# Third attention layer: raw keys loaded in a head's second step; score operands and value tables of later heads issued by GpSimd

## The chip, the cores and the metric

One core of one Trainium2 chip runs the whole program. The metric is the device time of one execution in microseconds (us). Durations in the traces are in us unless they are marked ns.

## The reference, cut to what is touched

The program is a chain of four attention layers and four feed-forward layers on `x` of shape (4, 512, 128). The change lies in the third attention layer alone, which has 16 heads of 8 channels over 4 batches of 512 tokens, and a bias and a value term that depend on the clipped distance between query and key:

```python
qkv = (x @ w_qkv.T).reshape(B, N, 3, H, hd).transpose(2, 0, 3, 1, 4)
q, k, v = (qkv[0] * scale, qkv[1], qkv[2])
attn = jnp.einsum('bhid,bhjd->bhij', q, k)
idx = rp[None, None]                       # clip(j - i, -31, 31) + 31
qL = jnp.einsum('bhid,hdm->bhim', q, rpe_k_table)
attn = attn + jnp.take_along_axis(qL, idx, axis=-1)
kL = jnp.einsum('bhjd,hdm->bhjm', k * scale, rpe_q_table)
attn = attn + jnp.swapaxes(jnp.take_along_axis(kL, idx, axis=-1), 2, 3)
attn = jax.nn.softmax(attn, axis=-1)
out = jnp.einsum('bhij,bhjd->bhid', attn, v)
S = segment_sum of attn over rp            # 63 sums for each query
out = out + jnp.einsum('inbh,hnd->bhid', S, rpe_v_table)
return x_out @ w_proj.T + b_proj
```

## The kernel before

The layer (`l2_attn`, L2053) has a preparation and then a loop over 16 heads. A head has 8 steps; a step is one pair of blocks of 32 queries, for all 4 batches at once, on 128 partitions. Each engine runs its own program in order, written out by the Python loop over `t` = 8h + i, where h is the head and i the step (0 to 7). The engines are held together by semaphores alone. What each engine does, by step:

- TensorE: `scores(t)` (bf16 parts of queries and keys, 51 rows, at the start of each step), then `key_bands(h + 1, i - 1)` in steps 1 to 3 (the key bias of the next head, from `xk` and `kshift`), `query_bands(h + 3, i - 4)` in steps 4 to 7, the value matmuls of the half head before in three parts, and `relative(n)` (L2708) four steps later.
- VectorE: `maximum(t)` (adds the bias of `qb`, takes the row maximum), `turn` (transposes probabilities), in steps 3 and 7 `turn_band` (L2534, transposes the band `sb` of the half head that ended four steps before step 4 or 0) and `normalize`.
- ScalarE: evacuation of the key and query bands, `exp(t)`, `outputs`.
- GpSimd: `sums` and `cut` (L2474, masks `sb`) every fourth step, `combine(h + 1)` in step 4 (4.7 us of work on `qb`: the DMA-loaded query bias and the key bias `kb` of the next head), `values(h + 1)` in step 5 (the value operand `vd`; waits for the value matmuls of the half head before, whose last part is in TensorE's step 4), `expand(h + 2)` in step 7 (L2457, spreads the raw keys `rawk` into `xk`).
- SyncE issues every DMA of the loop. In its order of a head: `q_load(h + 1)` (skewed read of the query band from HBM into `qb`, 768 KB) and `q_store(h + 2)` (768 KB to HBM) in step 0; `p_store` in steps 0, 2, 4 and 6 (probability bands of two steps to HBM, 736 KB a head, in rows of 384 bytes or less); `s_load` in steps 3 and 7 (L2399, the stored band read back skewed into `sb`, 384 KB each), which first waits until the two stores that it reads have landed; `head_scores(h + 1)` in step 3 (query parts 192 KB, key parts 384 KB, bias rows 24 KB); `keys(h + 2)` in step 4 (raw keys, 8 rows of 8 KB each read 16 times, 1024 KB, and `kshift`, 56 KB); `head_values(h)` in step 5 (48 KB).

The skewed reads have this access pattern, whose outermost dimension is the 4 batches:

```python
def skewed(band, offset, step, width):
    pitch = width + GRP
    return bass.AP(band.tensor, band.offset + offset, [[GRP * pitch, B], [pitch + step, GRP], [1, width]])
```

`keys(h)` waits for `xk_ready` >= h, that is, until `expand(h - 1)` has read the one `rawk` tile. `expand(h)` needs the load and the last key round of head h - 1 (step 3). The first key round of head h + 1, in TensorE's step 1, waits for `expand(h + 1)`. `combine(h + 1)` has to be done when VectorE starts head h + 1.

Of the kernel before, what the change touches and what calls it, by code (L numbers as in the profile page):

```python
# [12 lines left out]
P = 128  # L13
# [4 lines left out]
T = B * NT  # L18
# [4 lines left out]
HEADS, HD = 16, 8  # L23
# [2029 lines left out]
def l2_attn(nc, xs, c, w, scratch):  # L2053
# [4 lines left out]
    with ExitStack() as ctx:  # L2058
# [15 lines left out]
        ps_l = s.ps("ps_l", [P, N])  # L2074
        names = ("w_loaded t_loaded m_loaded rv_loaded zero_ready zeroed wt_ready wT_ready zb_ready t_ready zT_ready qk_ps base_ready hi_ready res_ready "
                 "mid_ready lo_ready q_lo gam_ps gam_ready g_lo g_stored v_ps va_ready tab_ready tab_stored rvd_ready rvd_stored st0 st1 "
                 "ones_ready once_ready hl0 hl1 kl kt0 kt1 rl0 rl1 l_ps l_ready qw0 qw1 qw2 qr0 qr1 pw0 pw1 pw2 sr0 sr1 tabq_ready "
                 "s_ps biased nm_ready p_ready tT xk_ready added comb_ready sm_ready vs_ready masked st_ready vd_ready pv_done o_ps oe_ready u_ps rr_ready o_done "
                 "at_ps aoT_ready y_ps y_ready dve")
        m = {n: s.sem(n) for n in names.split()}  # L2080
        ident = c["ident"]
        head_loaded = [m["hl0"], m["hl1"]]
        shifts_loaded = [m["kt0"], m["kt1"]]
        rv_slot_loaded = [m["rl0"], m["rl1"]]
        qband_read = [m["qr0"], m["qr1"]]
# [242 lines left out]
        with nc.Block() as block:  # L2328
            @block.sync
            def _(sp):  # L2330
# [22 lines left out]
                def head_values(h):  # L2353

                    if h >= 2:
                        sp.wait_ge(m["o_ps"], 2 * h - 2)
                    sp.dma_start(rvt[h % 2][:, :, :].rearrange("p k n -> p (k n)"), rv_d[h]).then_inc(rv_slot_loaded[h % 2], 16)
# [61 lines left out]
                for t in range(L2_STEPS + 4):  # L2419
                    h, i = t // PAIRS, t % PAIRS  # L2420
                    if t % 2 == 0 and 0 <= (t - 2) // 2 < L2_STEPS // 2:
                        p_store((t - 2) // 2)
                    if t % 4 == 3 and 0 <= (t - 7) // 4 < 2 * HEADS:
                        s_load((t - 7) // 4)
                    if i == 0 and h + 1 < HEADS:
                        q_load(h + 1)
                    if i == 0 and 3 <= h + 2 < HEADS:
                        q_store(h + 2)
                    if i == 3 and 2 <= h + 1 < HEADS:
                        head_scores(h + 1)  # L2430
                    if i == 4 and h + 2 < HEADS:
                        keys(h + 2)
                    if i == 5 and 2 <= h < HEADS:
                        head_values(h)

            @block.gpsimd
            def _(g):
                g.memset(ones3[:, :], 1.0).then_inc(m["ones_ready"], 1)
                g.memset(xk[:, 0:GRP], 0.0).then_inc(m["once_ready"], 1)
                g.memset(xk[:, GRP + T * P:], 0.0).then_inc(m["once_ready"], 1)  # L2440
# [52 lines left out]
                for t in range(L2_STEPS + 12):  # L2493
                    h, i = t // PAIRS, t % PAIRS
                    if t % 4 == 1 and 0 <= (t - 5) // 4 < 2 * HEADS:
                        sums((t - 5) // 4)
                    if t % 4 == 2 and 0 <= (t - 10) // 4 < 2 * HEADS:
                        cut((t - 10) // 4)
                    if i == 4 and h + 1 < HEADS:
                        combine(h + 1)  # L2500
                    if i == 5 and 2 <= h + 1 < HEADS:
                        values(h + 1)
                    if i == 7 and h + 2 < HEADS:
                        expand(h + 2)
                ln.powers(g, 2 * B, start=B)

# [123 lines left out]
            def _(pe):  # L2630
# [22 lines left out]
                def scores(g):  # L2653
                    h, slot = g // PAIRS, g % 2
                    if g % PAIRS == 0:
                        pe.wait_ge(head_loaded[h % 2], 16 * (HEAD_LOADS * (h // 2 + 1) + 1))
                    if g >= 2:
                        pe.wait_ge(m["p_ready"], 2 * g - 2)
                    r0 = P // 2 * (h % 2)
                    for u in range(2):  # L2660
                        a = 2 * (g % PAIRS) + u
                        right = GRP * (a - 1) if a else 0
                        for b in range(B):
                            out = ps_s[slot][GRP * b:GRP * (b + 1), u, :]
                            q = qs[r0:r0 + FROWS, b * N + GRP * a:b * N + GRP * (a + 1)]
                            keys = lambda v, lo, hi: ks[r0:r0 + FROWS, v, b * N + lo:b * N + hi]
                            if a == 0:
                                pe.matmul(out[:, 0:GRP], q, keys(0, N - GRP, N), start=True, stop=True)
                                last = pe.matmul(out[:, GRP:N], q, keys(0, 0, N - GRP), start=True, stop=True)
                            else:  # L2670
                                if right:
                                    pe.matmul(out[:, N - right:N], q, keys(1, 0, right), start=True, stop=True)
                                last = pe.matmul(out[:, 0:N - right], q, keys(0, right, N), start=True, stop=True)  # L2673
                    last.then_inc(m["s_ps"], 1)
# [33 lines left out]
                def relative(n):  # L2708
# [1 line left out]
                    h = n // 2  # L2710
                    pe.wait_ge(m["st_ready"], n + 1)
                    if n % 2 == 0:
                        pe.wait_ge(rv_slot_loaded[h % 2], 16 * (h // 2 + 1))
                    for k in range(3):
                        last = pe.matmul(ps_o[n % 2][GRP * k:GRP * (k + 1), :], rvt[h % 2][:, k, :], st[n % 2][:, :, k, :], start=False, stop=True)
                    last.then_inc(m["o_ps"], 1)
# [570 lines left out]
```

## Time and profile before

| | |
|---|---|
| median of 3 runs | 2629.41 us (2624.09 to 2635.16) |
| the profiled execution | 2632.55 us |
| its span, first to last instruction | 2630.6 us |
| mean granted TensorE clock | 0.849 |
| busy in the span: TensorE, VectorE, ScalarE, GpSimd | 1926.2, 1713.3, 1090.8, 847.6 us |
| head loop of this layer | 1610 to 2076 us of the span |

The profiled execution took 1.95 us more than its span. Busy times are shares of the whole program; for a change in one loop the table by stretches of that loop and the waits in it are what to read.

### The profile page before, as it was taken

To read this page: it belongs to the slowest core of one execution; us is meant where nothing else is said; L and a number is where in the kernel's file an instruction comes from. 1 tells how busy PE (TensorE), PEld (TensorE's weight loads), DVE (VectorE), ACT (ScalarE), POOL (GpSimd) and SP (SyncE) were. 2 spreads that over 40 slices of the span, in tenths; PEclk is the share of its full clock that TensorE was granted. 3 is DMA by queue.
4 is the path that set the end of the run, shared out by engine and by line. 5 is a ranking of instruction groups with operands and counts; after the bars stand their busy time and mean duration, and the time that the engine had idled before them with its cause. 6 is when DMAs were issued, how large, how long until landed. Compare 5 with 4: busy or idle time off the path is not lost. (4 is left out here: it accounts for less than half of the span.)

```text
span 2630.6 us, 46533 instructions
## 1 busy us (share of the span) xinstructions
PE 1926.2 (73%) x16472; PEld 1324.4 (50%) x16472; DVE 1713.3 (65%) x4060; ACT 1090.8 (41%) x2021; POOL 847.6 (32%) x627
## 2 busy tenths in 40 slices
PE   4888886387777784559999647787787549995446
PEld 1555554155555553437777524454454338884334
DVE  3777776576555554659999843788888672224564
ACT  1666663254544442204444223555555213331332
POOL 3000000574444421014444334445545169201001
PEclk8999999699999987659999765898988669997667
DMA  3011110210000000010000065566665140000000
GB/s 100 29 38 39 39 39 3 63 27 15 15 15 15 15 15 5 1 21 11 20 20 20 11 192 140 164 177 172 173 173 153 48 175 17 16 0 8 0 1 19
DMA packets 126467, 145.04 MB, mean 55 GB/s; under 512 B 72472, under 2 KB 100171, under 8 KB 123490
## 3 DMA queue, kind: packets, MB, share of 16 engines
q1 hardware_dynamic: 123040, 132.95, 18.1%
q10 hardware_dynamic: 3266, 9.96, 1.0%
q8 instruction: 99, 1.62, 0.3%
q14 instruction: 62, 0.51, 0.1%
HBM read 94.59 MB, written 40.81 MB: 51 GB/s over the span
## 5 line engine op out<-in xcount | busy, mean ns | idle before, releaser
L407 ACT ACTIVATE l0a_pr<-l0a_sm,l0a_nm 128x512 f32<-128x512 f32 x256 | 184.9, 723 | 147.4 <-DVE l0a_nm L324 146.9
L324 DVE CUSTOM_DVE_ANT_0 l0a_sm<-l0a_ps_s,l0a_tb 128x512 f32<-128x512 f32 x256 | 171.0, 685 | 93.9 <-PE l0a_ps_s L473 90.8
L2606 ACT ACTIVATE l2a_pr<-l2a_ps_s,l2a_nm 128x512 f32<-128x512 f32 x256 | 174.1, 687 | 120.8 <-DVE l2a_nm L2525 119.9
L481 PE MATMUL l0a_ps_p<-top_c_ident,l0a_pr 128*128 128x128 f32 x1024 | 170.4, 290 | 54.2 <-ACT l0a_pT L415 54.1
L481 PEld LDWEIGHTS l0a_ps_p<-top_c_ident,l0a_pr 128*128 128x128 f32 x1024 | 110.0, 143 | 117.1 <-ACT l0a_pr L407 64.7
L2525 DVE TENSOR_REDUCE l2a_nm<-l2a_ps_s 128x2 f32<-128x1024 f32 x128 | 156.7, 1224 | 4.4
L2532 DVE STREAM_TRANSPOSE l2a_tt<-l2a_pr 128x1024 f32<-128x1024 f32 x128 | 158.0, 1234 | 0.1
L1508 POOL TENSOR_TENSOR l1f_h<-l1f_lm,l1f_sg 128x512 f32<-128x512 f32 x72 | 92.6, 1286 | 184.0 <-DVE l1f_lm L1577 184.0
L754 POOL TENSOR_TENSOR l0f_ct<-l0f_raw,l0f_cos_scaled 128x1024 f32<-128x1024 f32 x32 | 76.3, 2386 | 184.1 <-issue 94.7
L1880 ACT ACTIVATE l2f_h<-l2f_ps_h 128x512 f32<-128x512 f32 x128 | 76.7, 599 | 134.7 <-PE l2f_ps_h L1425 128.9
L1635 ACT ACTIVATE l1f_csb<-l1f_ps_c,l1f_b3e 128x512 f32<-128x512 f32 x128 | 88.2, 689 | 104.9 <-PE l1f_ps_c L1425 104.6
L1918 PEld LDWEIGHTS l2f_ps_y<-l2f_w2T,l2f_h 128*128 128x128 f32 x1024 | 119.1, 192 | 2.6
L2702 PE MATMUL l2a_ps_o<-l2a_tt,l2a_vd 128*32 128x256 f32 (+7 forms) x1472 | 119.8, 364 | 0.0
L1918 PE MATMUL l2f_ps_y<-l2f_w2T,l2f_h 128*128 128x128 f32 x1024 | 119.3, 275 | 0.0
L1838 DVE SCALAR_TENSOR_TENSOR l2f_acc<-l2f_ps_y,l2f_comb,l2f_acc 128x128 f32<-128x128 f32 x112 | 31.6, 344 | 133.1 <-PE l2f_ps_y L1918 132.9
L990 PE MATMUL l0f_ps_side<-l0f_wqkv,l0f_hT 128*128 128x512 f32 x192 | 109.8, 663 | 11.5 <-ACT l0f_hT L905 10.8
L2523 DVE TENSOR_TENSOR l2a_ps_s<-l2a_ps_s,l2a_qb 128x192 f32<-128x192 f32 (+2 forms) x160 | 45.7, 303 | 106.2 <-PE l2a_ps_s L2673 61.3
L286 POOL COPY l0a_vh<-l0a_va 128x128 f32 x14 | 4.1, 296 | 333.2 <-PE l0a_ps_o L492 333.2
L473 PE MATMUL l0a_ps_s<-l0a_ks,l0a_qs 48*128 48x512 bf16 x256 | 101.7, 398 | 10.1 <-issue 9.5
L2649 PE MATMUL l2a_ps_l<-l2a_xk,l2a_kshift 128*32 128x256 f32 x768 | 71.3, 504 | 48.7 <-POOL l2a_xk L2462 46.2
L770 POOL TENSOR_TENSOR l0f_rn<-l0f_ss,top_c_half 128x16 f32<-128x16 f32 x32 | 95.0, 2968 | 33.1 <-DVE l0f_ss L854 32.1
L2462 POOL TENSOR_TENSOR l2a_xk<-l2a_rawk,l2a_masks 128x2048 f32<-128x2048 f32 x16 | 72.3, 4517 | 66.0 <-DMA l2a_rawk<-l_k 66.0
(501 smaller groups left out, 5220.9 us busy)
## 6 DMA issues: line engine op xcount, KB each, us to landing
l2a_rawk<-l_k SPq DMA_DIRECT2D x16, 1024.0 KB, 13.2
l2a_qb<-l_qband SPq DMA_DIRECT2D x16, 768.0 KB
l2a_sb<-l_pband SPq DMA_DIRECT2D x32, 384.0 KB
l_qband<-l2a_staged SPq DMA_DIRECT2D x14, 768.0 KB, 15.4
l0a_tb<-l_bias SPq DMA_DIRECT2D x16, 448.0 KB
l2a_ks<-l_k SPq DMA_DIRECT2D x16, 384.0 KB
l_pband<-l2a_pr SPq DMA_DIRECT2D x32, 192.0 KB, 9.4
l_pband<-l2a_pr SPq DMA_DIRECT2D x32, 144.0 KB, 2.9
```

What stands on the lines that cost most here:

```text
L324: v.tensor_tensor_reduce(sm[j % 4][:, :], ps_s[j % 2][:, :], tb[slot][:, off:off + N][:, ::-1], -1.0, 3e38, ALU.add, ALU.min, nm[:, j % 4: ...
L407: a.activation(pr[j % 4][:, :], sm[j % 4][:, :], ACT.Exp, bias=nm[:, j % 4:j % 4 + 1], scale=-1.0).then_inc(m["p_ready"], 1)
L473: pe.matmul(ps_s[j % 2][:, :], qs[slot][:, b * N + it * P:b * N + (it + 1) * P], ks[slot][:, b * N:(b + 1) * N], start=True, stop=True).th ...
L481: last = pe.transpose(ps_p[j % 2][:, tile(k)], pr[j % 4][:, tile(k)], ident[:, :])
L770: g.tensor_tensor(rn[:, u, :], ss[:, u, :], c["half"][:, :], ALU.pow).then_inc(m["rn_ready"], 1)
L990: last = pe.matmul(bank[:, :], hT[:, tile(t)], wqkv[:, l, i * F_INNER:(i + 1) * F_INNER], start=True, stop=True)
L1508: g.tensor_tensor(h[b % 2][:, k, :], lm[:, k, :], sg[:, k, :], ALU.mult).then_inc(h_ready, 1)
L1918: last = pe.matmul(ps_y[b % 2][:, t, :], h[b % 2][:, k, t * P:(t + 1) * P], w2T[slot][:, k, :], start=(k == 0), stop=(k == FC - 1))
L2525: v.tensor_reduce(nm[:, g % 2, :], ps_s[g % 2][:, :, :], AX, ALU.max, negate=True).then_inc(m["nm_ready"], 1)
L2532: v.transpose(tt[n % 2][:, u * NB:(u + 2) * NB, :].rearrange("p (u k) i -> p u (k i)", u=2), pr[g // 2 % PR_RING][:, 2 * (g % 2):2 * (g % ...
L2606: a.activation(pr[slot][:, 2 * (g % 2) + u, :], ps_s[g % 2][:, u, :], ACT.Exp, bias=nm[:, g % 2, u:u + 1], accum_out=rs[:, n % 2, 2 * (g % ...
L2702: last = pe.matmul(ps_o[n % 2][GRP * g:GRP * (g + 1), (lo - a0) * GRP:(hi - a0) * GRP], vd[h % 2][:, v, k, :], tt[n % 2][:, block:block + ...
```

## The change

`keys(h + 2)` moves on SyncE from step 4 to step 1. `head_scores` and `head_values` leave SyncE's loop (the calls for heads 0 and 1 ahead of it stay). GpSimd issues the same four transfers for heads 2 to 15: `score_loads(h + 1)` in its step 2 (three DMAs) and `value_load(h)` in its step 4, with semaphores of their own and the same conditions. GpSimd's own work moves too: `values(h + 1)` from step 5 to step 3, `combine(h + 1)` from 4 to 5, `expand(h + 2)` from 7 to 6. TensorE waits for the new semaphores in heads 2 and later.

```diff
@@ -2074,12 +2074,14 @@
         ps_l = s.ps("ps_l", [P, N])
         names = ("w_loaded t_loaded m_loaded rv_loaded zero_ready zeroed wt_ready wT_ready zb_ready t_ready zT_ready qk_ps base_ready hi_ready res_ready "
                  "mid_ready lo_ready q_lo gam_ps gam_ready g_lo g_stored v_ps va_ready tab_ready tab_stored rvd_ready rvd_stored st0 st1 "
-                 "ones_ready once_ready hl0 hl1 kl kt0 kt1 rl0 rl1 l_ps l_ready qw0 qw1 qw2 qr0 qr1 pw0 pw1 pw2 sr0 sr1 tabq_ready "
+                 "ones_ready once_ready hl0 hl1 gh0 gh1 gv0 gv1 kl kt0 kt1 rl0 rl1 l_ps l_ready qw0 qw1 qw2 qr0 qr1 pw0 pw1 pw2 sr0 sr1 tabq_ready "
                  "s_ps biased nm_ready p_ready tT xk_ready added comb_ready sm_ready vs_ready masked st_ready vd_ready pv_done o_ps oe_ready u_ps rr_ready o_done "
                  "at_ps aoT_ready y_ps y_ready dve")
         m = {n: s.sem(n) for n in names.split()}
         ident = c["ident"]
         head_loaded = [m["hl0"], m["hl1"]]
+        later_head_loaded = [m["gh0"], m["gh1"]]
+        later_rv_loaded = [m["gv0"], m["gv1"]]
         shifts_loaded = [m["kt0"], m["kt1"]]
         rv_slot_loaded = [m["rl0"], m["rl1"]]
         qband_read = [m["qr0"], m["qr1"]]
@@ -2426,15 +2428,26 @@
                         q_load(h + 1)
                     if i == 0 and 3 <= h + 2 < HEADS:
                         q_store(h + 2)
-                    if i == 3 and 2 <= h + 1 < HEADS:
-                        head_scores(h + 1)
-                    if i == 4 and h + 2 < HEADS:
+                    if i == 1 and h + 2 < HEADS:
                         keys(h + 2)
-                    if i == 5 and 2 <= h < HEADS:
-                        head_values(h)
 
             @block.gpsimd
             def _(g):
+                def score_loads(h):
+
+                    g.wait_ge(m["s_ps"], PAIRS * (h - 1))
+                    first, sem = P // 2 * (h % 2), later_head_loaded[h % 2]
+                    g.dma_start(qs[first:first + KROWS, :], q3[h * HD:(h + 1) * HD].rearrange("d c t -> (d c) t")).then_inc(sem, 16)
+                    g.dma_start(ks[first:first + KROWS, :, :].rearrange("p v t -> p (v t)"),
+                                k3[h * HD:(h + 1) * HD].rearrange("d c v t -> (d c) (v t)")).then_inc(sem, 16)
+                    src = bass.AP(g3.tensor, g3.offset + h * 3 * T * P, [[T * P, 3], [HEADS * 3 * T * P, 2], [1, T * P]])
+                    g.dma_start(ks[first + KROWS:first + FROWS, :, :], src).then_inc(sem, 16)
+
+                def value_load(h):
+
+                    g.wait_ge(m["o_ps"], 2 * h - 2)
+                    g.dma_start(rvt[h % 2][:, :, :].rearrange("p k n -> p (k n)"), rv_d[h]).then_inc(later_rv_loaded[h % 2], 16)
+
                 g.memset(ones3[:, :], 1.0).then_inc(m["ones_ready"], 1)
                 g.memset(xk[:, 0:GRP], 0.0).then_inc(m["once_ready"], 1)
                 g.memset(xk[:, GRP + T * P:], 0.0).then_inc(m["once_ready"], 1)
@@ -2496,11 +2509,15 @@
                         sums((t - 5) // 4)
                     if t % 4 == 2 and 0 <= (t - 10) // 4 < 2 * HEADS:
                         cut((t - 10) // 4)
-                    if i == 4 and h + 1 < HEADS:
+                    if i == 2 and 2 <= h + 1 < HEADS:
+                        score_loads(h + 1)
+                    if i == 3 and 2 <= h + 1 < HEADS:
+                        values(h + 1)
+                    if i == 4 and 2 <= h < HEADS:
+                        value_load(h)
+                    if i == 5 and h + 1 < HEADS:
                         combine(h + 1)
-                    if i == 5 and 2 <= h + 1 < HEADS:
-                        values(h + 1)
-                    if i == 7 and h + 2 < HEADS:
+                    if i == 6 and h + 2 < HEADS:
                         expand(h + 2)
                 ln.powers(g, 2 * B, start=B)
 
@@ -2653,7 +2670,9 @@
                 def scores(g):
                     h, slot = g // PAIRS, g % 2
                     if g % PAIRS == 0:
-                        pe.wait_ge(head_loaded[h % 2], 16 * (HEAD_LOADS * (h // 2 + 1) + 1))
+                        pe.wait_ge(head_loaded[h % 2], 16 * (HEAD_LOADS + 1))
+                        if h >= 2:
+                            pe.wait_ge(later_head_loaded[h % 2], 16 * HEAD_LOADS * (h // 2))
                     if g >= 2:
                         pe.wait_ge(m["p_ready"], 2 * g - 2)
                     r0 = P // 2 * (h % 2)
@@ -2710,7 +2729,9 @@
                     h = n // 2
                     pe.wait_ge(m["st_ready"], n + 1)
                     if n % 2 == 0:
-                        pe.wait_ge(rv_slot_loaded[h % 2], 16 * (h // 2 + 1))
+                        pe.wait_ge(rv_slot_loaded[h % 2], 16)
+                        if h >= 2:
+                            pe.wait_ge(later_rv_loaded[h % 2], 16 * (h // 2))
                     for k in range(3):
                         last = pe.matmul(ps_o[n % 2][GRP * k:GRP * (k + 1), :], rvt[h % 2][:, k, :], st[n % 2][:, :, k, :], start=False, stop=True)
                     last.then_inc(m["o_ps"], 1)
```

## Rows read from the trace of the kernel before

**Rows 1.** The page's groups of instructions, line engine op, out<-in.

```profile
L2649 PE MATMUL l2a_ps_l<-l2a_xk,l2a_kshift 128*32 128x256 f32 x768 | 71.3, 504 | 48.7 <-POOL l2a_xk L2462 46.2 <-ACT l2a_kb L2592 1.4 <-ACT l2a_pr L2585 0.6
...
L2462 POOL TENSOR_TENSOR l2a_xk<-l2a_rawk,l2a_masks 128x2048 f32<-128x2048 f32 x16 | 72.3, 4517 | 66.0 <-DMA l2a_rawk<-l_k 66.0
```

**Rows 2.** Waits, 1660 to 2060 us: total us, times, longest us.

```profile
PE l2a_ps_s L2668 <- DMA l2a_ks<-l_g: 17.7, 9, 6.7
```

**Rows 3.** Waits of SyncE's queue, 1560 to 2100 us.

```profile
SPq L2403 <- DMA l_pband<-l2a_pr: 65.0, 15, 9.5
```

**Rows 4.** Table by stretches; the last three columns are clock, DMA share, GB/s.

```profile
1669.94:2011.30 341.36, 272.17 (x3952) 159.41 (x3952) 283.02 (x380) 180.12 (x484) 165.75 (x120) 0.87 0.63 173
1678.00:1679.00 1.00, 1.00 (x20) 0.19 (x16) 0.00 (x0) 0.00 (x0) 0.00 (x0) 0.50 0.21 61
1789.00:1790.00 1.00, 0.00 (x0) 0.00 (x0) 1.00 (x2) 0.00 (x0) 1.00 (x1) 0.50 0.98 402
1794.00:1795.00 1.00, 1.00 (x20) 0.36 (x16) 0.37 (x1) 1.00 (x4) 0.00 (x0) 0.50 0.25 104
1832.00:1840.00 8.00, 7.79 (x124) 5.51 (x120) 7.90 (x10) 5.08 (x14) 6.13 (x6) 1.00 0.98 214
```

**Rows 5.** SyncE's timeline over one head: start, duration of the issue.

```profile
1812.99 0.53 SPq L2404 DMA_DIRECT2D l2a_sb<-l_pband  x1
...
1814.68 0.53 SPq L2380 DMA_DIRECT2D l2a_qb<-l_qband  x1
1815.31 1.64 SPq L2373 DMA_DIRECT2D l_qband<-l2a_staged  x1
...
1825.24 0.52 SPq L2404 DMA_DIRECT2D l2a_sb<-l_pband  x1
1825.81 1.43 SPq L2347 DMA_DIRECT2D l2a_qs<-l_q  x1
...
1831.08 0.39 SPq L2397 DMA_DIRECT2D l_pband<-l2a_pr  x1
1831.51 0.57 SPq L2336 DMA_DIRECT2D l2a_rawk<-l_k  x1
...
1837.64 0.37 SPq L2397 DMA_DIRECT2D l_pband<-l2a_pr  x1
1840.97 0.54 SPq L2404 DMA_DIRECT2D l2a_sb<-l_pband  x1
```

**Rows 6.** SyncE's timeline: loads of step 7 of heads 0, 1, 13; a long issue.

```profile
1635.61 0.55 SPq L2404 DMA_DIRECT2D l2a_sb<-l_pband  x1
...
1648.99 7.06 SPq L2347 DMA_DIRECT2D l2a_qs<-l_q  x1
...
1669.94 0.53 SPq L2404 DMA_DIRECT2D l2a_sb<-l_pband  x1
...
2011.30 0.54 SPq L2404 DMA_DIRECT2D l2a_sb<-l_pband  x1
```

**Rows 7.** GpSimd's timeline over the same head as rows 5.

```profile
1829.67 1.28 POOL L2470 TENSOR_TENSOR l2a_qb<-l2a_qb,l2a_masks 128x512 f32<-128x512 f32 x1 [8.63 <-ACT l2a_kb L2592]
1831.03 3.45 POOL L2472 TENSOR_TENSOR l2a_qb<-l2a_qb,l2a_kb 128x1536 f32<-128x1536 f32 x1
...
1834.64 0.72 POOL L2448 TENSOR_TENSOR l2a_vs<-l2a_va,l2a_rvf 128x256 f32<-128x256 f32 x1
1835.44 2.04 POOL L2452 TENSOR_TENSOR l2a_vd<-l2a_vs,l2a_masks 128x512 f32<-128x512 f32 x2
1838.70 0.73 POOL L2477 TENSOR_TENSOR l2a_sb<-l2a_sb,l2a_masks 128x256 f32<-128x256 f32 x1 [1.23 <-DMA l2a_sb<-l_pband]
1843.46 4.52 POOL L2462 TENSOR_TENSOR l2a_xk<-l2a_rawk,l2a_masks 128x2048 f32<-128x2048 f32 x1 [4.02 <-DMA l2a_rawk<-l_k]
```

**Rows 8.** Last head, empty queue: SyncE's issue of a band load.

```profile
2059.19 0.52 SPq L2404 DMA_DIRECT2D l2a_sb<-l_pband  x1
```

**Rows 9.** GpSimd's `cut` that waited for the load of rows 8.

```profile
2066.10 0.73 POOL L2477 TENSOR_TENSOR l2a_sb<-l2a_sb,l2a_masks 128x256 f32<-128x256 f32 x1 [1.72 <-DMA l2a_sb<-l_pband]
```

## The prediction

> **What bounds the kernel now.** I read the groups of instructions first, then the waits of all engines, the waits of SyncE's queue, the table by stretches of 1 us, and last the timelines of SyncE and GpSimd over one head. The groups show what the change seems made for: TensorE stands 46.2 us in front of its key rounds until `expand` is done, and GpSimd stands 66.0 us in front of `expand` until the raw keys have landed [rows 1]. TensorE also waits 17.7 us for the key parts of the scores [rows 2]. SyncE waits 65.0 us in `s_load` for its own stores to land [rows 3]. Three transfers late at once point at the transfers themselves.
>
> The table by stretches gives the reason. A DMA share of 0.25 with 104 GB/s is 4 of the 16 DMA engines at full speed, 26 GB/s each; all sixteen reach 402 GB/s, 25 each [rows 4]. The skewed reads (`q_load`, `s_load`) have 4 as their outermost dimension and show just this share. Over the 390 windows of 1 us from 1645 to 2035 us the share never falls below 0.21; the lowest is shown [rows 4]. So four DMA engines are never idle through heads 1 to 13, while the other twelve often are. Head by head the step-7 `s_load` is issued every (2011.30 - 1669.94) / 12 = 28.45 us [rows 6]. That is the four engines' work of one head. VectorE, the busiest compute engine, has 283.02 / 12 = 23.6 us of work a head in the same stretch [rows 4].
>
> The rule behind the 4 is in the Trainium skill, DMA: Bandwidth & Descriptors, section "Why a DMA increments its semaphore by 16 and not by 1": a transfer is spread over the largest number up to 16 that divides the slowest dimension of both sides. The trace agrees (0.25).
>
> What the four engines move in a head, from the sizes in the text above: a quarter of 768 + 2 x 384 KB = 384 KB, and a sixteenth of 768 + 1024 + 600 + 736 + 56 + 48 = 3232 KB, 202 KB. At 26 GB/s (393 + 207 thousand bytes) this is 15.1 + 8.0 = 23.1 us. The other 28.45 - 23.1 = 5.35 us are lost where all sixteen run at once and well below 402 GB/s: 214 GB/s at a share of 0.98 from 1832 to 1840 us [rows 4], just behind the issue of the raw keys [rows 5].
>
> **The change part by part.** No byte is removed and none is added. The question for each part is thus what it does to four engines that are always busy.
>
> *Raw keys in step 1.* Now they are last in line: issued at 1831.51, 18.5 us into the cycle that begins with the `s_load` at 1812.99, landed at 1843.46, 2.5 us after the next cycle began at 1840.97 [rows 5, 7]. Issued in step 1 they stand right behind `q_store` (1815.31), and land long before GpSimd wants them. But `expand` stands in GpSimd's order behind `cut`, and `cut` needs the step-3 `s_load`, issued at 1825.24 and landed at 1838.70, 25.7 us into the cycle [rows 5, 7]. This `s_load` had 2.5 us of the head before's raw keys ahead of it in the line; now it has this head's. It lands at the same point. `expand` can then start at 25.7 + 0.73 instead of 30.5 and end 4 us sooner, so TensorE's wait for `xk` (46.2 us in all, some 3.3 a head [rows 1]) goes. What is late next is `cut` itself: `turn_band` in VectorE's step 7 needs it, and then the `p_store` of step 4, for which SyncE stands in step 7. The 3.3 us move there.
>
> *What stands behind that store.* The store issued at 1831.08 frees SyncE at 1840.97 [rows 5]. Until then and for 2.5 us after, the four engines have the raw keys behind it and never run dry. After the change only the step-6 store (1837.64) is behind it, 192 KB over sixteen engines, 12 thousand bytes each, 0.5 us at 26 GB/s and some 0.9 at the pace of the crowded stretch (214 / 16). A hole opens: landing of the store, issue of `s_load`, its first bytes. Its size comes from the last head, where the line is empty: `s_load` issued at 2059.19, `cut` at 2066.10, 6.9 us for 384 KB that take 3.8 us at 104 GB/s [rows 8, 9]. So 3.1 us of start and landing for one transfer; covered by 0.9, the hole is at most 2.2 us. It is 0 where something else still stands in line. I take 0.7 a head, a third, since the overhead's parts also overlap and part of the 5.35 us may go when the crowd falls elsewhere; ends 0 and 2.2.
>
> *The crowded stretch.* Raw keys on twelve engines will now run beside `q_load` on the four instead of beside `s_load`. Both are the same kind of skewed read, so I keep the 5.35 us; ends: all of it goes, or none.
>
> *Score operands and value tables on GpSimd.* SyncE is freed of issues of 1.43 us and shorter, in one case 7.06 us, which delayed the stores of head 1 behind it [rows 5, 6]. Head 1's cycle was 1669.94 - 1635.61 = 34.3 us, 5.9 above the others; I count this as won. TensorE's 17.7 us for the key parts go (the loads are issued in step 2 and do not queue behind SyncE's), but they lie inside the 28.45 and are no gain of their own. GpSimd gets four issues a head. No row shows its DMA issue; by SyncE's rows it is 0.5 to 1.5 us each, 2 to 6 us on an engine with 165.75 / 12 = 13.8 us of work a head [rows 4]: hidden by its idle time. If an issue were 5 us it would not be (below).
>
> The Trainium skill speaks against this part (DMA: Bandwidth & Descriptors, "Issuing engines are not separate DMA queues"): transfers of all issuers run on the same 16 engines, and a second issuer saves only issue time. By the rule the steady cycle stays at 28.45 us; a reader who took the waits as gain would sum 46.2 + 17.7 = 64 us. The rows above side with the rule.
>
> *GpSimd's order.* `values(h + 1)` in step 3 has to wait for the value matmuls of TensorE's step 4, so `values`, one issue, `sums`, `combine`, `cut` and `expand` run one behind the other: 0.72 + 2.04 + 1 + 1.28 + 3.45 + 0.73 + 4.52 = 13.7 us [rows 7], about 14 with the small `sums`, from step 4 on. TensorE wants `xk` in the next head's step 1. From that step to the end of step 4 are some 3.5 steps, 10.5 us at 23.6 / 8 a step. The floor of a head is therefore near 25 us, below 28.45, so this order costs nothing while the four DMA engines bind.
>
> *Ends.* Head 14 has no raw keys, head 15 nothing to load: no term.
>
> **Sum.** 12 heads x 0.7 = +8.4; head 1: 0.7 - 5.9 = -5.2. Together +3.2 on the 2632.55 us of the profiled execution, 2635.8. That execution lay 3.1 above the median, so 2633 for the median.
>
> **Rivals.** *The waits were real.* If the crowded stretch shrinks, the cycle falls to 26.5 us, midway between the floor of 25 and today's 28.45 (the bytes alone need 23.1): 12 x -1.95 - 7.9 = -31, 2598. At the floor: 12 x -3.45 - 9.3 = -51, 2579. For it: 5.35 of 28.45 us are not bytes at full speed. Against: nothing in the change removes the crowd, it only moves it. Chance 0.30.
>
> *The hole.* On the other side: the line of the four engines runs dry for the full 2.2 us each head. 12 x 2.2 + 2.2 - 5.9 = +22.7, 2652. It decides as soon as less than 2 us of work stands behind the step-4 store when it lands; the order of SyncE's program says just that. Against it: GpSimd's transfers are not in SyncE's line and may fall into the hole. Chance 0.18.
>
> *GpSimd as issuer.* If an issue took it 5 us instead of 1, the three score loads need 15 us between `cut` of step 2 (about 7 us into the cycle) and the value matmuls of step 4 (about 20), 2 too many, and the chain of 14 becomes 18, some 2 beyond what the cycle leaves: +4 a head, +50, about 2680. Point of decision: 4 us an issue. Chance 0.05.
>
> **The numbers.** My forecast holds with 0.47. Within 0.5% (13 us, about what a measurement of this kernel can tell from no change) fall 0.36 of it and 0.06 of the rivals' inner ends: 0.42. Faster by more: 0.28 of the first rival and 0.02 of my own lower end: 0.30. Slower: 0.14 of the hole, 0.05 of GpSimd as issuer and 0.09 of my own upper end: 0.28. The range takes in both ends of the hole and most of the first rival: 2592 to 2658. For my own case alone it is 2620 to 2647.
>
> **What would show it.** Right: the DMA share stays at or above 0.2 nearly everywhere, with short dips once a head behind the step-7 `s_load`; the cycle of `s_load` is 28 to 30 us; TensorE's wait for `xk` and for the key parts is near 0; VectorE waits instead for `cut` before `turn_band`, some 3 us a head; head 1's cycle is near 29. Wrong: a cycle under 27 us with the crowded stretch shorter or faster; or a GpSimd whose issues of several us stand between its operations. I would also be wrong if the four engines' share were not one line: if transfers from GpSimd's queue could run on other engines than the busy four.

## The result: 3.2% slower, and the profile after

The changed kernel takes 2714.81 us (median of 4 runs, 2709.68 to 2717.96) beside 2629.04 us for the kernel before on the same chip (4 runs, 2624.09 to 2635.16). The ratio is 1.0323, interval 1.0294 to 1.0352: 85.8 us slower. I had forecast 2633 and a range up to 2658.

The profiled execution took 2709.68 us, 77.1 above that of before. First where they lie: SyncE's timeline, the step-7 `s_load` of heads 0, 1 and 13, and between them one of step 3 (kernel after; start, duration of the issue).

```profile
1630.06 0.55 SPq L2406 DMA_DIRECT2D l2a_sb<-l_pband  x1
...
1642.08 6.70 SPq L2406 DMA_DIRECT2D l2a_sb<-l_pband  x1
...
1665.09 0.54 SPq L2406 DMA_DIRECT2D l2a_sb<-l_pband  x1
...
2087.99 0.54 SPq L2406 DMA_DIRECT2D l2a_sb<-l_pband  x1
```

Beside [rows 6]: head 0 comes 5.55 us sooner, head 1's cycle is 35.0 instead of 34.3, and the twelve cycles behind it take (2087.99 - 1665.09) / 12 = 35.24 us instead of 28.45. That is -5.55 + 0.7 + 12 x 6.79 = +76.6 of the 77.1. The -5.55 is no gain of the change. The layer itself starts 6.97 us sooner in this execution, after stages that the change doesn't touch (VectorE's first row of the layer, before and after):

```profile
1498.73 0.88 DVE L2007 BATCH_NORM_STATS2 l2a_ln_stats<-top_xs 128x6 f32<-128x128 f32 x4 [1.14 <-PEq L53]
```

```profile
1491.76 0.87 DVE L2007 BATCH_NORM_STATS2 l2a_ln_stats<-top_xs 128x6 f32<-128x128 f32 x4 [1.15 <-PEq L53]
```

From there to head 0's load it takes 138.3 us instead of 136.9. Without the early start the two spans differ by 84.3 us, near the 85.8 of the medians. So the question is one of a single cycle: why 6.8 us more?

The groups that answer to [rows 1], from the kernel after:

```profile
L2666 PE MATMUL l2a_ps_l<-l2a_xk,l2a_kshift 128*32 128x256 f32 x768 | 63.7, 459 | 11.5 <-POOL l2a_xk L2475 7.8 <-ACT l2a_kb L2609 2.2 <-ACT l2a_pr L2602 0.6
```

```profile
L2475 POOL TENSOR_TENSOR l2a_xk<-l2a_rawk,l2a_masks 128x2048 f32<-128x2048 f32 x16 | 72.4, 4524 | 9.0 <-DMA l2a_rawk<-l_k 9.0
L2490 POOL TENSOR_TENSOR l2a_sb<-l2a_sb,l2a_masks 128x256 f32<-128x256 f32 x32 | 23.3, 729 | 109.0 <-DMA l2a_sb<-l_pband 109.0
```

The waits, 1660 to 2160 us, all engines (total us, times, longest us), kernel after:

```profile
ACT l2a_pr L2623 <- DMA l_pband<-l2a_pr: 130.6, 14, 12.0
...
PE l2a_ps_s L2687 <- ACT l2a_pr L2623: 108.6, 13, 10.5
POOL l2a_sb L2490 <- DMA l2a_sb<-l_pband: 107.2, 30, 7.2
...
POOL l2a_vs L2461 <- PE l2a_ps_o L2721: 81.5, 13, 7.7
POOL l2a_qb L2483 <- DMA l2a_qb<-l_qband: 73.2, 13, 7.9
...
DVE l2a_st L2555 <- POOL l2a_sb L2490: 29.7, 16, 4.4
```

The change does what it says: TensorE's 46.2 us for `xk` [rows 1] are 7.8, GpSimd's 66.0 us for the raw keys are 9.0 (its wait for the bands in front of `cut` is 109.0), and in the window of the waits no line of TensorE names `xk` or the key parts of [rows 2]. In their place GpSimd and ScalarE wait for other transfers of the four-engine line, and TensorE and VectorE for ScalarE. The largest wait is one that I had not listed at all: `exp` of step 6 wants a buffer of its ring of three, and the store of step 2 that must free it has not landed.

SyncE's timeline over one head (kernel after), to be read beside [rows 5]:

```profile
1807.25 0.54 SPq L2406 DMA_DIRECT2D l2a_sb<-l_pband  x1
...
1808.94 0.57 SPq L2382 DMA_DIRECT2D l2a_qb<-l_qband  x1
1809.61 1.19 SPq L2375 DMA_DIRECT2D l_qband<-l2a_staged  x1
1811.82 0.86 SPq L2338 DMA_DIRECT2D l2a_rawk<-l_k  x1
...
1815.71 0.32 SPq L2393 DMA_DIRECT2D l_pband<-l2a_pr  x1
1816.07 0.44 SPq L2394 DMA_DIRECT2D l_pband<-l2a_pr  x1
1816.62 11.76 SPq L2406 DMA_DIRECT2D l2a_sb<-l_pband  x1
1828.42 6.37 SPq L2399 DMA_DIRECT2D l_pband<-l2a_pr  x2
1842.52 0.54 SPq L2406 DMA_DIRECT2D l2a_sb<-l_pband  x1
```

GpSimd's timeline over the same head (idle time and its releaser in brackets), beside [rows 7]:

```profile
1814.36 0.74 POOL L2490 TENSOR_TENSOR l2a_sb<-l2a_sb,l2a_masks 128x256 f32<-128x256 f32 x1 [2.37 <-DMA l2a_sb<-l_pband]
1815.04 0.54 POOL L2440 DMA_DIRECT2D l2a_qs<-l_q  x1
1815.57 0.53 POOL L2441 DMA_DIRECT2D l2a_ks<-l_k  x1
1816.10 0.59 POOL L2444 DMA_DIRECT2D l2a_ks<-l_g  x1
...
1825.70 0.60 POOL L2449 DMA_DIRECT2D l2a_rvt<-l_rv  x1
...
1832.94 1.26 POOL L2483 TENSOR_TENSOR l2a_qb<-l2a_qb,l2a_masks 128x512 f32<-128x512 f32 x1 [6.36 <-DMA l2a_qb<-l_qband]
...
1841.84 0.72 POOL L2490 TENSOR_TENSOR l2a_sb<-l2a_sb,l2a_masks 128x256 f32<-128x256 f32 x1 [4.15 <-DMA l2a_sb<-l_pband]
1842.52 4.53 POOL L2475 TENSOR_TENSOR l2a_xk<-l2a_rawk,l2a_masks 128x2048 f32<-128x2048 f32 x1
```

The issues on GpSimd are short, 0.5 to 0.6 us. The `s_load` of step 3 is not: SyncE stands in its issue for 11.76 us, where before it took 0.52 [rows 5], and the two stores behind it another 6.37. My reading is that the line takes no more until it has worked some off. And `expand` starts the moment `cut` is done (1842.52): the raw keys have long landed, as forecast, and it is `cut` that is late.

Table by stretches (kernel after; clock, DMA share, GB/s in the last columns), beside [rows 4]:

```profile
1807.00:1808.00 1.00, 0.00 (x0) 0.00 (x0) 0.66 (x1) 0.00 (x0) 1.00 (x2) 0.50 0.03 6
...
1816.00:1817.00 1.00, 1.00 (x25) 0.90 (x28) 1.00 (x2) 0.62 (x2) 0.69 (x2) 1.00 0.94 123
1823.00:1824.00 1.00, 1.00 (x20) 0.79 (x11) 1.00 (x2) 0.90 (x3) 0.92 (x2) 1.00 0.84 82
1842.00:1843.00 1.00, 0.00 (x0) 0.00 (x0) 0.40 (x1) 0.00 (x0) 1.00 (x2) 0.50 0.04 10
```

Two things are new: once a head the four engines run dry (a share of 0.03), and in the crowd all sixteen are busy and move little: 123 and 82 GB/s in the two windows shown, against 214 in [rows 4]. Over all windows of 1 us with a share above 0.7 in heads 1 to 12 the mean is 198 GB/s, against 242 before.

**A head in four pieces.** The comparisons below cut each cycle at four events of the timelines: the step-7 `s_load` is issued (S); GpSimd starts the `cut` of that band (B); it starts the first operation of `combine`, which wants the query band (Q); it starts the `cut` of the step-3 band (C); and the next S. In the head above: S 1807.25, B 1814.36, Q 1832.94, C 1841.84, S 1842.52. These are means over heads 1 to 12 of each trace, worked out from the starts of these rows:

| kernel | S to B | B to Q | Q to C | C to S | cycle | time, us |
|---|---|---|---|---|---|---|
| before | 7.5 | 8.9 | 9.5 | 2.5 | 28.45 | 2629 |
| after | 7.5 | 18.2 | 8.9 | 0.7 | 35.2 | 2715 |
| raw keys in step 1 alone | 7.4 | 13.7 | 10.7 | 2.4 | 34.3 | 2703 |
| no raw keys for later heads | 7.5 | 9.5 | 7.8 | 1.2 | 25.9 | 2593 |
| raw keys in step 3 | 7.1 | 9.3 | 10.5 | 5.2 | 32.1 | 2673 |
| halves, steps 1 and 4 | 7.2 | 11.8 | 10.0 | 2.5 | 31.5 | 2660 |
| distinct rows, step 4 | 7.4 | 9.2 | 8.5 | 2.3 | 27.45 | 2610 |
| distinct rows, step 1 | 7.5 | 10.7 | 11.1 | 2.4 | 31.7 | 2672 |
| later loads on GpSimd alone | 7.5 | 13.4 | 8.7 | 0.6 | 30.2 | 2655 |
| the same on ScalarE | 7.4 | 10.9 | 10.2 | 0.7 | 29.2 | 2640 |
| changed kernel, all on SyncE | 7.6 | 15.2 | 11.0 | 0.7 | 34.4 | 2699 |

GpSimd's rows tell when it uses a band. The semaphore updates in the traces tell when the band lands, and where GpSimd waits for it the two agree within 0.1 us. They part most in the kernel without later raw keys: there `cut` starts without a wait in all 12 heads, right behind `combine` and `values`. By the landings its pieces are 7.4, 9.5, 6.4 and 2.6 us, beside 7.4, 8.8, 9.6 and 2.6 before and 7.4, 13.7, 10.7 and 2.5 with the raw keys in step 1.

### The profile page after: what moved, and what is told of

Its sections match the earlier page's. It is cut to its first block and busy times, and to the rows that moved or that the text cites. A ratio compares the mean times of both kernels' runs of the same rounds, so it can differ in the third digit from the quotient of the medians.

```text
span 2707.9 us, 46533 instructions
## 1 busy us (share of the span) xinstructions
PE 1927.5 (71%) x16472; PEld 1324.2 (49%) x16472; DVE 1713.6 (63%) x4060; ACT 1089.2 (40%) x2021; POOL 877.5 (32%) x683
## 3 DMA queue, kind: packets, MB, share of 16 engines
q10 hardware_dynamic: 3266, 9.96, 1.0%
## 5 line engine op out<-in xcount | busy, mean ns | idle before, releaser
L1880 ACT ACTIVATE l2f_h<-l2f_ps_h 128x512 f32<-128x512 f32 x128 | 76.6, 599 | 135.2 <-PE l2f_ps_h L1425 129.1
L473 PE MATMUL l0a_ps_s<-l0a_ks,l0a_qs 48*128 48x512 bf16 x256 | 100.9, 395 | 10.2 <-issue 9.6
L770 POOL TENSOR_TENSOR l0f_rn<-l0f_ss,top_c_half 128x16 f32<-128x16 f32 x32 | 95.0, 2969 | 33.1 <-DVE l0f_ss L854 32.1
L2653 PE MATMUL l2a_ps_l<-l2a_tabq,l2a_q 128*128 128x96 f32 x512 | 85.8, 319 | 8.0 <-ACT l2a_pr L2602 3.4
L332 DVE COPY l0a_pT<-l0a_ps_p 128x512 f32<-128x512 f32 x128 | 87.8, 686 | 4.3 <-issue 3.5
```

The source lines that it names most:

```text
L473: pe.matmul(ps_s[j % 2][:, :], qs[slot][:, b * N + it * P:b * N + (it + 1) * P], ks[slot][:, b * N:(b + 1) * N], start=True, stop=True).th ...
L770: g.tensor_tensor(rn[:, u, :], ss[:, u, :], c["half"][:, :], ALU.pow).then_inc(m["rn_ready"], 1)
```

## The experiments

Each time is a median with its ratio to the kernel before, run beside it on the same chip (2626.5 to 2629.1 us).

**1. Raw keys alone.** The kernel before, with one step changed:

```
-                    if i == 4 and h + 2 < HEADS:
-                        keys(h + 2)
+                    if i == 1 and h + 2 < HEADS:
+                        keys(h + 2)
```

> The kernel before with one move: keys(h + 2) goes from step 4 to step 1 of SyncE's order; score operands and value tables stay with SyncE, GpSimd's order stays. Theory P (place of the raw keys): the loss of 85 us comes from the raw keys standing ahead of the stores and band loads in SyncE's line and beside the query band load; then this kernel alone loses most of it, 2690 to 2720 us, a cycle of the step-7 band load of 33 to 35 us, and ScalarE waits for stores as in the changed kernel. Theory G (GpSimd as issuer): transfers that GpSimd issues move slower and slow the others; then this kernel is within 15 us of before or, with a hole of up to 2 us a head, at most at 2655.

Measured: 2703.23 us, 1.0295 (1.0273 to 1.0317), +76. This lies in theory P's range, and the cycle of 34.3 too. One line of the change makes nearly all of the loss.

**2. Later loads on GpSimd alone.** The changed kernel with `keys` back in step 4, GpSimd's old order, and `value_load` in step 5.

> The other part alone: GpSimd issues the score operands in its step 2 and the value tables in step 5; the raw keys stay in step 4, and GpSimd's combine, values and expand stay in steps 4, 5 and 7. Theory P: near before, 2620 to 2645 us, cycle 28 to 29 us. Theory G: most of the 85 us, 2680 to 2720, with a stretch of over 10 us a head in which the DMA share is near 1 at about 140 GB/s.

Measured: 2655.38, 1.0112 (1.0082 to 1.0141), +28. It falls between the two theories. The 76 and the 28 overlap: together the change costs 86.

**3. The changed kernel, all loads on SyncE.** `score_loads` and `value_load` stand in SyncE's program in the same steps.

> The changed kernel with its four later loads issued by SyncE again, in the same steps 2 and 4, and with the same semaphores; raw keys in step 1 and GpSimd's new order stay. Theory P: as slow as the changed kernel or slower, 2700 to 2740, since the score operands now stand in the same line ahead of the step-3 band load. Theory G: 2625 to 2660.

Measured: 2698.78, 1.0276 (1.0256 to 1.0297), +72. Theory P comes nearest: the time lies just under its range. The issuer accounts for some 14 to 16 us of the loss, the places of the transfers for the rest.

**4 and 5. The skewed reads on sixteen engines.** Each skewed read becomes four transfers of 32 rows, in the kernel before and in the changed one:

```
-                    sp.dma_start(sb[n % 2][:, :, :].rearrange("p a n -> p (a n)"), skewed(pband[n % PBAND_RING], 1, 1, HROW)).then_inc(s_read[n % 2], 16)
+                    for b, src in enumerate(skewed(pband[n % PBAND_RING], 1, 1, HROW)):
+                        sp.dma_start(sb[n % 2][GRP * b:GRP * (b + 1), :, :].rearrange("p a n -> p (a n)"), src).then_inc(s_read[n % 2], 16)
```

> The kernel before with each skewed read (query band 768 KB, probability band 384 KB) issued as four DMAs, one for each batch, with 32 rows as the outermost dimension in place of 4; the semaphores count four times as much, nothing else changes. If four DMA engines set the pace, their work of 28.45 us a head falls, since the 384 KB a head that they moved alone (15.1 us) spread over sixteen (3.8 us): the cycle falls to what the engines need, about 25 us, the share of 0.25 is gone from the table, and the time is 2560 to 2590 us. If the compute engines or SyncE's waits set the pace and the low share is a symptom, the time stays within 10 us of before; SyncE issues nine more DMAs a head at 0.4 us.

> The changed kernel with each skewed read issued as four DMAs of 32 rows, one for each batch, as in the split version of the kernel before (2557.5 us). Theory F (the loss lives on the four DMA engines that alone carry the skewed reads): with those reads on sixteen engines the line has room, and this kernel is within 15 us of 2557. Theory O (GpSimd's new order or its issues cost time of their own): it stays 40 us or more above the split kernel before, 2600 to 2650.

Measured: 2557.53 for before with split reads, 0.9749 (0.9720 to 0.9778), and 2567.18 for the changed kernel with split reads, 0.9775 (0.9746 to 0.9804). The table by stretches of the first:

```profile
1700.00:1900.00 200.00, 169.78 (x2760) 105.79 (x2760) 195.73 (x269) 125.47 (x341) 114.41 (x83) 0.98 0.83 205
```

VectorE is now busy 195.73 of 200 us and the cycle is 24.1 us, and the first time lies just under its range. A share of 0.2 to 0.3 stands in 102 of the 342 windows of 1 us in heads 1 to 12 of the kernel before, and in 4 of 290 here (1645 to 1935 us). The line of the four engines was the bound. With it gone the whole change costs 9.7 us by the times, 7 by the two ratios, instead of 86: theory F. By the Trainium skill, DMA: Bandwidth & Descriptors, section "Why a DMA increments its semaphore by 16 and not by 1", a slowest dimension of 32 spreads over sixteen engines where one of 4 spreads over four. The trace agrees: before, each skewed read's semaphore rises in five updates, the last four when its data land; here each of the four transfers has sixteen. This version beats both kernels.

**6. GpSimd's new order alone.** The kernel before with `values` in step 3, `combine` in 5, `expand` in 6.

> The kernel before with GpSimd's own work in the changed kernel's steps: values in 3, combine in 5, expand in 6; all DMAs stay with SyncE in their old steps. The chain from the value matmuls to expand is 13.7 us of GpSimd's time and has to fit into some 15: if it does, the time is as before, 2620 to 2640. If the order alone delays the key rounds or the query bias, 2645 or more, with VectorE waiting for combine at a head's start.

Measured: 2630.69, 1.0008 (0.9997 to 1.0018). It costs nothing, as forecast.

**7 and 8. Raw keys from distinct rows.** The raw keys are eight rows of memory (64 KB) read sixteen times; here each partition has its own:

```
-                    src = bass.AP(k32.tensor, k32.offset + h * HD * T * P, [[0, HALF], [T * P, HD], [1, T * P]])
+                    src = bass.AP(k32.tensor, k32.offset, [[T * P, P], [1, T * P]])
```

> Raw keys alone in step 1 (2703 us), but the 1024 KB are read from 128 different rows of HBM, the channels of all heads, in place of this head's 8 rows 16 times each; the key bias is computed from other keys, so the output differs. Theory H (sixteen reads of the same 64 KB slow every DMA engine while they run, now the query band read too): the crowded stretch shrinks and the time falls by 30 us or more, to 2620 to 2670, query band landed less than 16 us after its issue. Theory L (the loss is the place in SyncE's line: the hole, and the stores that land late): same 2695 to 2710, query band landed 19 us after its issue.

> The kernel before, raw keys in step 4, but read from 128 different rows of HBM in place of 8 rows 16 times each; the key bias is computed from other keys, so the output differs. Theory H (reads of the same 64 KB by all engines cost time wherever they stand): faster than before by 10 to 35 us, 2595 to 2620. If they cost only beside the query band read: 2620 to 2635, as before.

Measured: 2671.92 with the keys in step 1, 1.0166 (1.0135 to 1.0197), 31 us less than with the repeated rows, though just above theory H's range (the query band lands 16.2 us after its issue, where it is 19.1 with the repeated rows and 14.0 before). And 2610.43 with the keys in step 4, 0.9942 (0.9924 to 0.9960), 19 us less, in theory H's range. Moving them still costs 61 us. So the repeated rows explain 13 to 15 of the 76 us, not more.

**9. Raw keys in step 3**, ahead of the score operands and behind the step-3 `s_load`.

> The kernel before with the raw keys in step 3 of SyncE's order: behind the step-2 store and the step-3 band load, ahead of the score operands. Theory H: the raw keys meet the band load, as before, not the query band read; 2625 to 2650. Theory L: the step-2 store no longer stands behind them, but the score operands and the step-4 store do and the hole opens: 2650 to 2680. Between the two on either side shows a mix.

Measured: 2673.04, 1.0177 (1.0147 to 1.0208), +45, in theory L's range. One step earlier already costs more than half of three. In the table the query band is nearly untouched (9.3 beside 8.9 us); it is C to S that doubles, to 5.2, with 1.0 more from Q to C.

**10. The later loads issued by ScalarE** instead of GpSimd, otherwise as experiment 2.

> As the kernel in which GpSimd alone issues the score operands in step 2 and the value tables in step 5, raw keys in step 4 (2655 us), but ScalarE issues these four loads in the same steps, behind its exponentials. Theory S (what costs is that GpSimd's software writes the descriptors): back to 2620 to 2640 us. Theory Q (what costs is a second queue that takes turns with SyncE's on the same DMA engines): 2645 to 2665. ScalarE's own issue time, four times some 0.6 us a head, is hidden, since it waits over 4 us a head.

Measured: 2640.17, 1.0043 (1.0024 to 1.0062), +12. This is the upper end of theory S and well below theory Q. Of the 28 us, 15 go with GpSimd as the issuer and 12 with a second queue and the earlier place; no run separates these two. The queues of the page (packets, MB, share of 16 engines), first with GpSimd as the issuer:

```profile
q1 hardware_dynamic: 119106, 123.65, 17.1%
q0 software_dynamic: 2912, 9.29, 1.7%
```

and with ScalarE:

```profile
q1 hardware_dynamic: 119106, 123.65, 16.8%
q10 hardware_dynamic: 7200, 19.26, 2.4%
```

ScalarE's queue has 9.96 MB and 1.0% in the kernel before, so the 9.3 MB took 1.4% here, 1.7% from GpSimd, and 2.0% in the changed kernel.

**11. Half of the raw keys in step 1, half in step 4.** The aim was to keep something behind the step-4 store.

```
+                    if i == 1 and h + 2 < HEADS:
+                        half_keys(h + 2, 0)
...
                     if i == 4 and h + 2 < HEADS:
-                        keys(h + 2)
+                        half_keys(h + 2, 1)
```

> The kernel before with the raw keys in two DMAs of 512 KB, the first 1024 columns in step 1, the rest in step 4 as before. If the raw keys' place acts through a hole behind the step-4 store (some 1.7 us a head without cover) and through the stretch beside the query band read (some 3.5 us a head more than before with all of them there), then half of them behind the store close most of the hole and the rest shrinks by half: a cycle of 30.2 to 30.8 us, 2650 to 2660 us, no window below 0.2. If what counts were only that GpSimd gets the whole tile late, it would be as before, 2620 to 2640. If any raw keys ahead of the stores cost the full price: 2690 to 2705.

Measured: 2660.30, 1.0125 (1.0108 to 1.0142), +31. The time fits the forecast, the cycle of 31.5 us lies above it, and some windows do fall below 0.2, the lowest to 0.11. The four engines ran dry for 3.0 us of 378 in heads 1 to 12 (windows of 1 us, a share s under 0.2 counted as 1 - s / 0.25), where experiment 1 has 21.4 of 412 and the kernel before 0. So with the hole nearly filled the loss is still 31 us, not far from half of the 76 for half of the keys (38). The dry time is not the loss.

**12. No raw keys at all for later heads.**

```
-                    src = bass.AP(k32.tensor, k32.offset + h * HD * T * P, [[0, HALF], [T * P, HD], [1, T * P]])
-                    sp.dma_start(rawk[:, :], src).then_inc(m["kl"], 16)
+                    if h < 2:
+                        src = bass.AP(k32.tensor, k32.offset + h * HD * T * P, [[0, HALF], [T * P, HD], [1, T * P]])
+                        sp.dma_start(rawk[:, :], src).then_inc(m["kl"], 16)
```

> The kernel before without the raw-key transfers of heads 2 to 15: every later head works on the raw keys of head 1, so its output is another one; all other transfers and all operations stay in their places. It gives the price of the raw keys in step 4, and with the 2703 us of the kernel that only moves them to step 1 their price there. A head is cut in four pieces: step-7 band load to its cut (7.5 us before, 7.5 with the keys in step 1), cut to combine (8.9 and 13.7), combine to the cut of the step-3 band (9.5 and 10.7), cut to the next band load (2.5 and 2.4). Theory A, the keys were filler: in step 4 they stand behind the step-3 band load and run in 4.8 us in which the four engines otherwise wait for the landing of the store, the next issue and its first bytes, and so cost next to nothing; in step 1 they stand ahead of both band reads of the head and are paid in full. Then without them the first and the last piece stay at 7.5 and 2.5, the cycle is 27.3 to 28.4 us and the time 2605 to 2629 us, and nearly all of the 76 us is their price in step 1. Theory B, the four engines never idle and every transfer costs its share: the cycle falls by 2.5 (bytes at full speed) to 4.8 us (at the crowded pace), 2567 to 2597 us, and the loss in step 1 has another cause on top.

Measured: 2592.85, 0.9869 (0.9837 to 0.9902), -34. The time is near the upper end of theory B's range, and the cycle, 25.9 us and so 2.5 less, is theory B's too. The raw keys cost 34 us in step 4 (2.5 in each of twelve cycles and 4.3 in head 1's) and 2703 - 2593 = 110 us in step 1 (8.4 in each cycle); the same 1024 KB, three times the price. Theory A holds for two pieces by the landings: 7.4 and 2.6 us with and without them, so what they reached into these two was free. It fails for the piece between the query band and the step-3 band, which is 6.4 us without them and 9.6 with them in step 4 (the piece before it is 0.8 shorter with them). Theory B's premise fails too: without the keys the four engines are dry for 15.5 of 312 us. The 34 us may be less than the keys' full price, since GpSimd comes 1.4 us late for the step-3 band in this kernel; no run tests that.

## Why the prediction was wrong

**The bound: right.** Four engines of sixteen set the cycle; the split reads (experiments 4 and 5) show it from both sides: -70 us for the kernel before, and the change's cost shrinks from 86 us to between 7 and 10.

**The waits named: right.** TensorE's waits for `xk` and for the key parts are gone and were worth nothing. GpSimd's issue takes 0.52 to 0.73 us, so the rival *GpSimd as issuer* is out in the form in which I gave it. VectorE waits for `cut` before `turn_band`, 29.7 us in 16 waits, about 2 a head where I said 3. GpSimd's order is free (experiment 6).

**"It lands at the same point": the step that failed.** Of the step-3 `s_load` I wrote that it had 2.5 us of the last head's raw keys ahead of it and now has this head's. That treats the line as a sum of bytes in which the order doesn't matter. From S to C it took 26.0 us before and takes 31.9 with the keys in step 1. This is all of the cycle's growth there (28.45 to 34.3). The runs show two reasons.

First, the 2.5 us ahead of the step-7 band were free, so that taking the keys away from there gave nothing back. S to B is 7.1 to 7.6 us in every kernel above, with raw keys reaching into it (before), without (experiment 1), and with none at all (experiment 12). An `s_load` in an empty line took 6.9 us [rows 8, 9], of which 3.8 are bytes. The raw keys lay in the other 3, and before that in the 2.5 us from C to S, in which SyncE waits for a store to land. In these two pieces they were filler. SyncE's timeline and the transfers of one head of experiment 1 show where they lie now; the second fence is the view of the transfers from 1805 to 1840 us (KB each, us from issue to landing), the third GpSimd's timeline.

```profile
1805.96 0.55 SPq L2404 DMA_DIRECT2D l2a_sb<-l_pband  x1
...
1809.84 0.55 SPq L2336 DMA_DIRECT2D l2a_rawk<-l_k  x1
...
1815.10 6.24 SPq L2404 DMA_DIRECT2D l2a_sb<-l_pband  x1
1821.39 6.82 SPq L2347 DMA_DIRECT2D l2a_qs<-l_q  x1
```

```profile
l2a_rawk<-l_k SPq DMA_DIRECT2D x1, 1024.0 KB, 22.6
```

```profile
1827.05 1.27 POOL L2470 TENSOR_TENSOR l2a_qb<-l2a_qb,l2a_masks 128x512 f32<-128x512 f32 x1 [13.25 <-DMA l2a_qb<-l_qband]
...
1837.01 0.72 POOL L2477 TENSOR_TENSOR l2a_sb<-l2a_sb,l2a_masks 128x256 f32<-128x256 f32 x1 [2.20 <-DMA l2a_sb<-l_pband]
```

The query band is there at 1827.05, the raw keys land at 1809.84 + 22.6 = 1832.4, the step-3 band at 1837.01. The keys stand between the two reads, for 5.4 us, and the band of 384 KB follows 4.6 us later. Before, they landed 4.8 us *behind* that band (1843.46 and 1838.70, [rows 7]). They slowed it there as well, but the whole price in step 4 was 2.5 us a cycle (experiment 12), and here it is 8.4.

Second, **"Both are the same kind of skewed read, so I keep the 5.35 us"** failed too. B to Q grows from 8.9 to 13.7 us, though the raw keys stand behind the query band in the line and land after it. The semaphore updates of this head show it: of the keys' sixteen parts twelve land by 1820.7 us, the query band's four at 1825.8 to 1827.0, and the keys' last four at 1830.4 to 1832.4. While the twelve run the keys, all sixteen are busy at 141 GB/s; then the four go on alone at nearly their full speed (experiment 1, table by stretches):

```profile
1813.00:1821.00 8.00, 7.72 (x134) 4.88 (x124) 7.53 (x11) 5.50 (x15) 0.74 (x1) 1.00 0.95 141
1821.00:1827.00 6.00, 5.79 (x89) 4.11 (x88) 5.93 (x8) 3.91 (x11) 0.00 (x0) 1.00 0.27 95
```

So my reading is that the keys on the other twelve slow the four; the views do not tell one transfer's packets from another's. In step 4 the keys do the same to the step-3 band (9.6 us instead of 6.4, experiment 12). A part of the loss is the repeated rows: with distinct rows B to Q grows only from 9.2 to 10.7. But Q to C then grows by 2.6 instead of 1.2, and the cycle still by 4.2. In the 1-us windows with a DMA share over 0.7 the sixteen moved 242 GB/s on average before and 214 in experiment 1; with distinct rows it was 266 and 246. Why repeated rows hurt more beside the query band than beside the step-3 band is not settled by these runs.

**The hole: right that it opens, wrong in what it costs.** The four engines are dry 1.8 us a head in experiment 1 (0.7 taken, 0 to 2.2 given) and 1.4 in the changed kernel. But the kernel without later raw keys is dry for 1.3 us a head and is 34 us *faster* than before, and experiment 11 has 0.25 and is 31 us slower. In experiment 1, S to B and C to S are as long as before. Dry time behind the store is a sign that filler was taken away; most of the price is paid where the filler was put.

**Score operands and value tables: mis-sized.** I took 0 for the steady cycle; alone they cost 28 us. Their place beside the query band and a second queue make 12 of it (B to Q 10.9 instead of 8.9, partly given back from C to S), and GpSimd as the issuer 15: B to Q 13.4. I had looked at the issue on the engine, which is short, and not at how the transfers then run. By the Trainium skill, DMA: Bandwidth & Descriptors, "Issuing engines are not separate DMA queues", a second issuer gains only issue time; the runs agree that nothing else is gained, and show 12 and 28 us lost on top.

**Head 1: wrong.** Its cycle was to fall from 34.3 to 29 and is 35.0. I had put its 5.9 us down to the one long issue of the score operands. The long issue did not go with them: it moved to the `s_load` of step 3 (6.70 us at 1642.08 in the first fence, 11.76 in the head shown, 6.24 in experiment 1). And in experiment 2, where no score operands stand in SyncE's loop, head 1's cycle is 34.7 us. It fell to 30.0 without its raw keys (experiment 12). What makes it longer than the others stays open.

**The sum.** Cycle +6.8 us where I had +0.7: in the order of the table, S to B 0, B to Q +9.3, Q to C -0.7, C to S -1.8. Twelve such cycles, head 1's +0.7, +1.4 ahead of head 0's load and +0.6 behind head 13's are the 84.3 us. The range ended at the full hole, 2652 and a little; no case in it let a transfer cost more than its bytes and the hole.

## What to carry to other kernels

In a line that never ran empty, the place of a transfer made its price: 1024 KB cost 2.5 us a head behind the last read that anyone waited for, and 8.4 ahead of it. Before moving a load earlier, ask which transfers it is now in front of, and what waited in the gap that it leaves. And where a DMA share stands at a quarter, look at the outermost dimension of the access pattern first: splitting those reads gave 70 us, more than any order of the loads.

## What the runs showed of the hardware

- An issue on SyncE can stall: 11.76, 6.82, 6.37 (two stores) and 6.24 us where the same instructions otherwise take 0.4 to 1.5. It is not the order alone that decides which: the kernel before has one row over 3 us in this loop, the same order without the later raw keys thirteen, the changed kernel 28. That a full line is the cause is my reading; no run measured how much it holds.
- The parts of one transfer land far apart: twelve of the raw keys' sixteen by 1820.7 us, the last at 1832.4 (experiment 1), since four engines have the skewed reads ahead of them.
- Reading the same eight rows sixteen times is slower than reading 128 distinct ones: 19 us over the kernel with sixteen such loads of 1024 KB, 31 where they run beside the query band.
- The same 9.3 MB took 1.4% of the engines' time from ScalarE's queue, 1.7 to 2.0% from GpSimd's software queue, with 15 us between the two kernels.
- An `s_load` took 7.1 to 7.6 us from its issue to its use as a mean in eleven kernels (single heads 6.8 to 9.3), for 384 KB that take 3.8 us at the 104 GB/s of [rows 4]. So some 3.5 us of it are an estimate of start and landing.
